# Attention and mixture of experts on one core: maxima ten steps ahead, moved inside SBUF, query rows loaded by half, expert weights and rows apart

## The chip, the cores and the metric

The kernel runs on one core of a Trainium2 chip. The metric is the device time of one execution in microseconds, lower is better.

## The reference, cut to what matters

Layer norm of x (2 x 1024 x 128), then two branches on the normed rows, both added to x: attention with 16 heads of 8 channels whose keys and values come from a latent of 32 channels, and a feed-forward with 16 experts of which each row takes its best two.

```python
def reference(...):
    q = (x @ Wq + bq).reshape(B, S, H, Dh)
    latent = x @ Wl + bl
    k = (latent @ Wk + bk).reshape(B, S, H, Dh)
    v = (latent @ Wv + bv).reshape(B, S, H, Dh)
    scores = jnp.einsum('bihd,bjhd->bhij', q, k) * SCALE
    attn = jax.nn.softmax(scores, axis=-1)
    out = jnp.einsum('bhij,bjhd->bihd', attn, v).reshape(B, S, D) @ Wo + bo
    ...
    top_vals, top_idx = jax.lax.top_k(logits, TOPK)
    gate = jnp.minimum(gate, LIMIT)
    up = jnp.clip(up, -LIMIT, LIMIT)
    gated = (up + 1.0) * gate * jax.nn.sigmoid(gate * ALPHA)
    out_e = jnp.einsum('tef,efh->teh', gated, Wd) + bd[None]
    return x + out + jnp.einsum('teh,te->th', out_e, cw)
```

## The kernel before

Everything is written by hand for the five engines, with semaphores. The sizes: batch 2, 1024 positions, 4 head groups of 4 heads for each batch, so 8 groups. A turn takes two groups; there are 4 turns. A unit is one group and one half (512) of its query positions; it has 8 steps, one for each block of 128 keys. So a turn has 4 units, 32 steps and 16 pairs of steps. The groups alternate between two buffers, q_rows0/k_rows0 (units 0 and 1 of a turn) and q_rows1/k_rows1 (units 2 and 3).

Setup. The projections give q2 and k2, each split into a high and a low part (`low_q`, `low_k`). The first group's rows are copied from them inside SBUF (`first_rows`, L323 ff.: SyncE for q, GpSimd for k). SyncE stores all parts to DRAM (`store_parts`, L393 ff.) and later loads each group from there (`load_group`, L381 ff.). VectorE works out the place of each row among its expert's blocks, GpSimd scatters the rows to a table in DRAM, and SyncE loads blocks of them back (`load_rows`, L374) and the weights of their experts (`load_weights`, L368 to L370, where expert numbers are read from SBUF into registers). Four blocks of 128 rows are a group of blocks; 12 of these are worked through, 4 to a turn.

The two rows with the maxima. Softmax needs each query's maximum before the exponentials. A row tile has 64 partitions, of which 62 hold parts of q and the last 2 (from MAXROW = 62) hold the negative maxima in two parts, against ones in k_rows. So a score product of 64 rows gives score minus maximum. The maxima come from products of 62 rows (`max_job`, L982) that run LEAD steps ahead of the scores, four to a step, through a ring of three PSUM banks: TensorE makes 128 x 512 scores, VectorE reduces them (L818). After the last maximum of a unit VectorE splits the maxima (L822 to L827, tile max2), TensorE turns them (`turn_maxima`, L988), VectorE copies them to maxT (L832), and two DMAs follow: `store_max` (L337) writes maxT to a DRAM buffer, `load_max` (L343) waits for that and loads it into rows 62 and 63 of q_rows. The first score product of a unit waits for this (s_maxin).

The main loop. `pair(p)` on each engine writes out two steps a and b. On TensorE, in this order: scores a0, two maxima, scores a1, a maximum, values of step a - 1 (L999), a maximum, scores b0, a maximum, then the turned blocks and one item of the experts' work (L1068 rows, L1070 gate, L1072 up, L1074 down), a maximum, scores b1, two maxima, values of step a. ScalarE makes an exponential from each of the four scores (L681) and copies the item's result. Pair numbers run from 3 to 18 in each turn's loop (HEAD = 3); 0 to 2 of the first turn stand ahead of it, and 16 to 18 are pairs 0 to 2 of the next turn. The last turn has no items, and its maxima end with the last step. In its pairs 10 to 15 the output projection is written.

What sets the order of the DMAs: SyncE's queue is one list, `turn(t)`, L429 ff. At pair p it has, in this order, the maxima (if a unit's are turned in p), a group load at p = 8 and 16 (it waits for the scores that use the buffer), first-turn weights and stores, and by the table RELOAD the next weights and rows of the experts, where the rows wait for the scatters of the buffer's last results. The first unit's maxima, and those turned in pairs 0 to 2, are moved by ScalarE's queue instead.

```python
LEAD = 12
RELOAD = {HEAD: (-2,), 5: (-1,), 11: (0,), 13: (1,)}
def has_max_turn(p, last):
    return p % 4 == 2 and has_max(p - 1, last)
```

## Time and profile before

| | |
|---|---|
| median of 3 runs | 473.39 us (470.63 to 473.43) |
| the profiled execution | 474.39 us, span 472.6 us |
| busy share of the span | TensorE 93%, VectorE 81%, ScalarE 65%, GpSimd 43% |
| mean granted TensorE clock | 0.94 |
| DMA | 38.05 MB, mean 81 GB/s |

The span is the time from the first to the last instruction on the chip; the execution's own time is a little longer. PE is TensorE, PEld its weight loads, DVE VectorE, ACT ScalarE, POOL GpSimd, SP SyncE; a q behind a name (SPq) means the engine's queue, where DMAs are issued. Matrix products are pipelined and overlap in the records. An engine that is idle costs nothing unless another waits for it.

### The profile page before, as it was taken

Reading aid. Unit: us, or ns where it says so; the run is one execution under the profiler, and the core shown is the slowest. Engines: PE = TensorE matmul, PEld = TensorE weight load, DVE = VectorE, ACT = ScalarE, POOL = GpSimd, SP = SyncE. Lnnn points to the kernel's source line nnn. Section 1 sums busy time; section 2 is a strip of 40 time slices with the busy share of each in tenths; the row PEclk is TensorE's granted clock in tenths of the full one; section 3 lists DMA queues with packets and bytes.
Section 4 is the critical chain, followed back from the end, with each engine's and each line's share of the span. In section 5 each row is a group of like instructions: output and inputs, shape, how many; then the busy total and the mean of one; then the engine's idle time right before and its main releaser. Section 6 shows DMA issues by size and latency. Waiting matters only on the chain.

```text
span 472.6 us, 9064 instructions
## 1 busy us (share of the span) xinstructions
PE 439.6 (93%) x2681; PEld 206.6 (44%) x2681; DVE 381.1 (81%) x757; ACT 309.2 (65%) x356; POOL 204.0 (43%) x238
## 2 busy tenths in 40 slices
PE   0998999989999989999999989999999999999995
PEld 0555444334444435444444444444444443333453
DVE  8559998958888887989898979898989888996112
ACT  1524005558777777787878777788787867676871
POOL 7043787205154543733454527442717274860000
PEclk9968555979999999999999999999999999999999
DMA  5994721464242315060503252513200322400001
GB/s 150 188 151 185 122 59 51 133 188 153 83 111 68 111 48 85 25 186 3 92 17 112 80 86 38 163 35 68 36 6 10 58 33 56 129 3 3 25 22 46
DMA packets 37699, 38.05 MB, mean 81 GB/s; under 512 B 5408, under 2 KB 33158, under 8 KB 36776
## 3 DMA queue, kind: packets, MB, share of 16 engines
q1 hardware_dynamic: 33696, 32.75, 30.4%
q0 software_dynamic: 2944, 4.75, 3.9%
q10 hardware_dynamic: 1032, 0.23, 0.3%
q8 instruction: 12, 0.20, 0.2%
q14 instruction: 15, 0.12, 0.1%
HBM read 23.77 MB, written 13.93 MB: 80 GB/s over the span
## 4 chain that ended last, share of the span: by engine, by line
PE 54%; DVE 18%; DMA 12%; ACT 6%; issue 5%; SPq 4%; ACTq 1%; DVEq 0%
PE banks L999 15%; DVE half_max L818 15%; PE banks L982 13%; PE banks L1051 11%; DMA k_rows<-k_parts 8%; ACT probs L681 5%; PE banks L1070 2%; SPq L389 2%; DMA max_rows<-maxT 2%; PE banks L1072 2%; PE banks L1007 1%; SPq L386 1%; PE banks L940 1%; PE banks L916 1%; DMA y<-in_x 1%
## 5 line engine op out<-in xcount | busy, mean ns | idle before, releaser
L818 DVE TENSOR_REDUCE half_max<-banks 128x1 f32<-128x512 f32 x512 | 322.2, 682 | 41.5 <-PE banks L982 40.1
L681 ACT ACTIVATE probs<-banks 128x1024 f32<-128x1024 f32 x256 | 254.1, 1024 | 122.5 <-PE banks L1051 115.1
L982 PE MATMUL banks<-k_rows,q_rows 62*128 62x512 f32 x512 | 181.5, 469 | 4.1 <-DVE half_max L818 2.4
L1051 PE MATMUL banks<-q_rows,k_rows 64*128 64x512 f32 x512 | 144.1, 460 | 9.8 <-ACT probs L681 3.3
L999 PE MATMUL banks<-probs,v_pad 128*32 128x512 f32 x1024 | 138.1, 612 | 0.1
L982 PEld LDWEIGHTS banks<-k_rows,q_rows 62*128 62x128 f32 x512 | 83.4, 197 | 89.8 <-DVE half_max L818 77.2
L1051 PEld LDWEIGHTS banks<-q_rows,k_rows 64*128 64x128 f32 x512 | 58.1, 189 | 78.8 <-ACT probs L681 63.1
L563 POOL DMA_INDIRECT moe_table<-x_rows,result_row x48 | 48.0, 999 | 64.4 <-ACT x_rows L669 46.9
L533 POOL TENSOR_TENSOR gate<-gate,w_blk 128x512 f32<-128x512 f32 x12 | 12.5, 1044 | 84.8 <-ACT gate L665 84.8
L523 POOL DMA_INDIRECT x_table<-xn,place_u x32 | 31.2, 976 | 22.6 <-DVE place_u L799 13.2
L999 PEld LDWEIGHTS banks<-probs,v_pad 128*32 128x32 f32 x1024 | 20.2, 108 | 43.0 <-issue 29.6
L533 POOL TENSOR_TENSOR up<-up,w_blk 128x512 f32<-128x512 f32 x12 | 12.6, 1047 | 9.4 <-ACT up L667 9.2
L551 POOL TENSOR_TENSOR up<-up,th 128x512 f32<-128x512 f32 x12 | 15.4, 1282 | 1.0
L546 POOL TENSOR_TENSOR th<-th,gate 128x512 f32<-128x512 f32 x12 | 15.3, 1273 | 1.0
L909 PE MATMUL banks<-id_f,xn 128*128 128x128 f32 x16 | 3.8, 412 | 12.5 <-DVE xn L738 12.5
L1070 PE MATMUL banks<-xT_blk,w_blk 128*128 128x128 f32 x96 | 13.9, 288 | 0.0
L1074 PE MATMUL banks<-w_blk,up 128*128 128x128 f32 x96 | 13.7, 286 | 0.0
L1070 PEld LDWEIGHTS banks<-xT_blk,w_blk 128*128 128x128 f32 x96 | 11.6, 191 | 4.4 <-ACT probs L681 4.1
L1074 PEld LDWEIGHTS banks<-w_blk,up 128*128 128x128 f32 x96 | 11.6, 191 | 3.3 <-ACT probs L681 3.3
L858 DVE TENSOR_TENSOR y<-y,banks 128x512 f32<-128x512 f32 x4 | 2.8, 688 | 12.5 <-PE banks L1035 12.5
L1072 PE MATMUL banks<-xT_blk,w_blk 128*128 128x128 f32 x96 | 12.7, 275 | 0.0
L1072 PEld LDWEIGHTS banks<-xT_blk,w_blk 128*128 128x128 f32 x96 | 11.7, 192 | 0.0
(119 smaller groups left out, 300.4 us busy)
## 6 DMA issues: line engine op xcount, KB each, us to landing
w_blk<-in_wexp SPq DMA_DIRECT2D x48, 193.0 KB, 2.7
q_rows<-q_parts SPq DMA_DIRECT2D x28, 128.0 KB
k_rows<-k_parts SPq DMA_DIRECT2D x56, 64.0 KB
x_table<-blank SPq DMA_DIRECT2D x1, 3096.0 KB, 19.9
x_rows<-x_table SPq DMA_DIRECT2D x12, 258.0 KB, 3.8
q_parts<-q SPq DMA_DIRECT2D x8, 256.0 KB
k_parts<-k SPq DMA_DIRECT2D x8, 256.0 KB
y<-in_x SPq DMA_DIRECT2D x4, 256.0 KB, 4.1
```

The lines of the kernel that those rows point to most:

```text
L523: pool.indirect_dma_start(x_table, bass.IndirectOffsetOnAxis(place_u[:, k, t:t + 1], 0), xn[:, t, :], None).then_inc(s_scattered, 16)
L533: mlp(nc.gpsimd.tensor_tensor(dst[:, :, :], dst[:, :, :], w_blk[:, GB * i:GB * i + GB, 2 * P + col:2 * P + col + 1].to_broadcast([P, GB, P ...
L551: nc.gpsimd.tensor_tensor(up[:, :, :], up[:, :, :], th[:, :, :], ALU.mult).then_inc(s_gated, 1)
L563: pool.indirect_dma_start(moe_table, bass.IndirectOffsetOnAxis(result_row[:, i, q:q + 1], 0), x_rows[:, i, q, 0:D], None, bounds_check=2 * ...
L681: nc.scalar.activation(probs[:, (2 * s + part) % 4, :, :], banks[:, bank:bank + 2, :], ACT.Exp, scale=SCALE).then_inc(slot_free, 1)
L818: nc.vector.tensor_reduce(half_max[:, unit, row, half:half + 1], banks[:, ring_bank(job), :], AX_X, ALU.max).then_inc(ring_free, 1)
L982: pe.matmul(bank, q_rows[slot][rows, pair, q0:q0 + P], k_rows[slot][rows, pair, 512 * keys:512 * keys + 512], start=True, stop=True).then_ ...
L999: mm = pe.matmul(banks[32 * j:32 * j + 32, 4, :], v_pad[:, (unit // 2) % 2, kb, j, :], probs[:, (2 * s + j // 2) % 4, j % 2, :], start=(kb ...
L1051: mm = pe.matmul(banks[:, bank + u, :], k_rows[(unit // 2) % 2][rows, pair, P * kb:P * kb + P], q_rows[(unit // 2) % 2][rows, pair, 512 * ...
L1070: mm = pe.matmul(block, w[:, 0:P], xT_blk[:, P * q:P * q + P], start=True, stop=True)
L1072: mm = pe.matmul(block, w[:, P:2 * P], xT_blk[:, P * q:P * q + P], start=True, stop=True)
L1074: mm = pe.matmul(block, up[:, q, :], w[:, 2 * P + 2:3 * P + 2], start=True, stop=True)
```

## The change

LEAD becomes 10. A unit's maxima are turned in the pair with p % 4 == 3, after its third maximum and directly ahead of the values, where before they were turned with p % 4 == 2 after the fifth. They go from maxT straight to q_rows by two DMAs within SBUF (`move_max`), one for each half of the partitions, and the DRAM buffer is gone. The tile q_rows has its half outermost, so that each half is loaded by itself and has its own semaphore (s_q1 for the second). The first group's q rows are copied half by half. TensorE waits for a group's rows one pair later. The weights of the first two groups of blocks are loaded ahead of the wait for the scatters and of the rows. RELOAD is split in two tables, WEIGHTS_IN and ROWS_IN, the rows one or two pairs after the weights. In the first turn, the second unit's maxima are moved by SyncE in pair 3 instead of by ScalarE in pair 2.

```diff
-LEAD = 12
+LEAD = 10
...
-RELOAD = {HEAD: (-2,), 5: (-1,), 11: (0,), 13: (1,)}
+WEIGHTS_IN = {HEAD: -2, 5: -1, 11: 0, 13: 1}
+ROWS_IN = {4: -2, 6: -1, 12: 0, 15: 1}
...
 def has_max_turn(p, last):
-    return p % 4 == 2 and has_max(p - 1, last)
+    return p % 4 == 3 and has_max(p - 1, last)
...
-TURN_OF_FIRST = 4 * KB + 4
+TURN_OF_FIRST = 4 * KB + 2
...
-        q_rows = [sb(f"q_rows{i}", [P, 2, S], F32R) for i in range(2)]
+        q_rows = [sb(f"q_rows{i}", [P, 2, 2, 512], F32R) for i in range(2)]
...
+        def move_max(queue, unit, job):
+
+            parity, slot, half = unit % 2, (unit // 2) % 2, unit % 2
             queue.wait_ge(ring_free, job + 1)
-            queue.dma_start(max_rows[unit % 2], maxT[:, unit % 2, :].bitcast(F32)).then_inc(s_maxout, 16)
-
-        def load_max(queue, unit, done):
-            parity, slot, half = unit % 2, (unit // 2) % 2, unit % 2
-            queue.wait_ge(s_maxout, 16 * done)
             for u in range(2):
-                queue.dma_start(q_rows[slot][64 * u + MAXROW:64 * u + ROWS, :, 512 * half:512 * half + 512].bitcast(F32),
-                                max_rows[parity, 16 * u:16 * u + 16].rearrange("(c j q) t -> c j (q t)", c=PARTS, j=2)).then_inc(s_maxin[parity], 16)
+                queue.dma_start(q_rows[slot][64 * u + MAXROW:64 * u + ROWS, half, :, :].bitcast(F32),
+                                maxT[16 * u:16 * u + 16, parity, :].bitcast(F32)).then_inc(s_maxin[parity], 16)
...
             def load_group(g, slot):
+                for half in range(2):
+                    for u in range(2):
+                        for c in range(PARTS):
+                            r = 64 * u + 2 * DH * c
+                            sp.dma_start(q_rows[slot][r:r + 2 * DH, half, :, :].bitcast(F32).rearrange("r j t -> r (j t)"),
+                                         q_parts[g, u, half].rearrange("a d j t -> (a d) (j t)")).then_inc((s_q1 if half else s_qk)[slot], 16)
+                            for a in range(PARTS * (1 - half)):
+                                sp.dma_start(k_rows[slot][r + DH * a:r + DH * a + DH, :, :].bitcast(F32).rearrange("r j t -> r (j t)"),
+                                             k_parts[g, u, c].rearrange("d j t -> d (j t)")).then_inc(s_qk[slot], 16)
...
             load_group(1, 1)
+            sp.wait_ge(s_expert, 1)
+            load_weights(0)
+            load_weights(1)
             sp.wait_ge(s_scattered, 16 * 2 * TILES)
             for m in range(SLOTS):
                 load_rows(m)
-            sp.wait_ge(s_expert, 1)
-            load_weights(0)
-            load_weights(1)
...
-            store_max(act, 0, TURN_OF_FIRST)
-            load_max(act, 0, 1)
+            move_max(act, 0, TURN_OF_FIRST)
             for p in range(HEAD):
                 pair(0, slots_before(p, 0, False), 0, p, False)
-                if has_max_turn(p, False):
-                    unit = (2 * p + LEAD - 2) // KB
-                    store_max(act, unit, AHEAD_JOBS + jobs_before(p, 0, False) + 5)
-                    load_max(act, unit, unit + 1)
...
-                if p == 2 and isinstance(t, int) and t == 0:
-                    pe.wait_ge(s_qk[1], qk_count(1, 0))
-                if p == 10 and not last:
+                if p == 3:
+                    pe.wait_ge(s_qk[1], qk_count(1, t))
+                if p == 7:
+                    pe.wait_ge(s_q1[1], q1_count(1, t))
+                if p == 11 and not last:
                     pe.wait_ge(s_qk[0], qk_count(0, t + 1))
-                if p == 18:
-                    pe.wait_ge(s_qk[1], qk_count(1, t + 1))
+                if p == 15 and not last:
+                    pe.wait_ge(s_q1[0], q1_count(0, t + 1))
```

The program of TensorE before, in pair 14 of the loop (each L1051 row is a score product, L982 a maximum, L999 values, a REGISTER_ALU row works out a wait's count). The turned maxima (L988) come after the fifth maximum, well behind the values:

```order
L982 MATMUL banks<-k_rows0,q_rows0 128x512 [waits ring_free]
L999 MATMUL banks<-probs,v_pad 32x512 [waits slot_free]
L999 MATMUL banks<-probs,v_pad 32x512 x3
L972 REGISTER_ALU
L982 MATMUL banks<-k_rows0,q_rows0 128x512 [waits ring_free]
L1040 REGISTER_ALU
L1051 MATMUL banks<-q_rows1,k_rows1 128x512 [waits slot_free]
L1051 MATMUL banks<-q_rows1,k_rows1 128x512
L972 REGISTER_ALU
L982 MATMUL banks<-k_rows0,q_rows0 128x512 [waits ring_free]
L986 REGISTER_ALU
L972 REGISTER_ALU [waits s_max2]
```

The row that follows these is the turned block itself, L988. And now, in pair 15 of the changed kernel (L1065 scores, L996 a maximum, L1002 the turned maxima, L1013 values):

```order
L1065 MATMUL banks<-q_rows1,k_rows1 128x512 [waits slot_free]
L1065 MATMUL banks<-q_rows1,k_rows1 128x512
L987 REGISTER_ALU
L996 MATMUL banks<-k_rows0,q_rows0 128x512 [waits ring_free]
L1000 REGISTER_ALU
L987 REGISTER_ALU [waits s_max2]
L1002 MATMUL banks<-id_f,max2 32x128 [waits ring_free]
L1013 MATMUL banks<-probs,v_pad 32x512 [waits slot_free]
L1013 MATMUL banks<-probs,v_pad 32x512 x3
```

The turned block moved from behind the fifth maximum of pair 14 to behind the third of pair 15, ahead of the values, and the unit's first scores stand at the start of pair 16 in both.

SyncE's queue before, at pairs 13 to 16, where x_rows is the experts' rows and max_rows the DRAM buffer:

```order
L370 DMA w_blk<-in_wexp 128x386
L374 DMA x_rows<-x_table 128x4x129 [waits s_res_out1]
L337 DMA max_rows<-maxT 32x128 [waits ring_free]
L343 DMA q_rows<-max_rows 2x2x512 [waits s_maxout]
L343 DMA q_rows<-max_rows 2x2x512
L386 DMA q_rows<-q_parts 16x2048 [waits slot_full]
```

And now:

```order
L380 DMA w_blk<-in_wexp 128x386
L353 DMA q_rows<-maxT 2x8x128 [waits ring_free]
L353 DMA q_rows<-maxT 2x8x128
L384 DMA x_rows<-x_table 128x4x129 [waits s_res_out1]
L398 DMA q_rows<-q_parts 16x1024 [waits slot_full]
```

The rows of the experts, and their wait for the scatters (s_res_out1), moved behind the maxima; one wait (s_maxout) between two DMAs is gone.

ScalarE's queue before, ahead of the loop (the first twelve exponentials are pairs 0 to 2):

```order
L337 DMA max_rows<-maxT 32x128 [waits ring_free]
L343 DMA q_rows<-max_rows 2x2x512 [waits s_maxout]
L343 DMA q_rows<-max_rows 2x2x512
L681 ACTIVATE probs<-banks 128x1024 [waits slot_full] x4
L681 ACTIVATE probs<-banks 128x1024 [waits s_pv,slot_full] x8
L337 DMA max_rows<-maxT 32x128 [waits ring_free]
L343 DMA q_rows<-max_rows 2x2x512 [waits s_maxout]
L343 DMA q_rows<-max_rows 2x2x512
```

And now:

```order
L665 ACTIVATE v_all<-banks 128x4x128 [waits s_v_ps] x4
L353 DMA q_rows<-maxT 2x8x128 [waits ring_free]
L353 DMA q_rows<-maxT 2x8x128
L698 ACTIVATE probs<-banks 128x1024 [waits slot_full] x4
L698 ACTIVATE probs<-banks 128x1024 [waits s_pv,slot_full] x8
```

The three DMAs behind pair 2 left this queue, and the wait for the store with them.

## Rows read from the trace of the kernel before

**Rows 1.** The page: busy time of an engine, share of the span, instructions.

```profile
PE 439.6 (93%) x2681; PEld 206.6 (44%) x2681; DVE 381.1 (81%) x757; ACT 309.2 (65%) x356; POOL 204.0 (43%) x238
```

**Rows 2.** A stretch of the steady part: busy time, granted clock, DMA share, GB/s.

```profile
200.00:220.00 20.00, 19.75 (x134) 8.91 (x134) 18.12 (x34) 16.51 (x20) 8.36 (x10) 1.00 0.39 112
```

**Rows 3.** Waits of TensorE for DMAs: us in all, times, longest.

```profile
PE banks L1051 <- DMA k_rows<-k_parts: 2.9, 5, 0.7
PE banks L1051 <- DMA q_rows<-max_rows: 2.8, 2, 1.4
```

**Rows 4.** ScalarE's timeline (start, length): first exponentials of pairs 2 to 5.

```profile
87.40 1.94 ACT L681 ACTIVATE probs<-banks 128x1024 f32<-128x1024 f32 x2 [1.34 <-PE banks L1051]
...
96.35 2.86 ACT L681 ACTIVATE probs<-banks 128x1024 f32<-128x1024 f32 x3 [3.66 <-DVE half_max L818]
...
103.75 1.94 ACT L681 ACTIVATE probs<-banks 128x1024 f32<-128x1024 f32 x2 [2.08 <-PE banks L1051]
...
110.06 1.94 ACT L681 ACTIVATE probs<-banks 128x1024 f32<-128x1024 f32 x2 [0.71 <-PE banks L1051]
```

**Rows 5.** Timelines of the lead: VectorE's maxima, first maxima moved, first scores.

```profile
43.32 19.22 DVE L818 TENSOR_REDUCE half_max<-banks 128x1 f32<-128x512 f32 x32
...
66.10 0.34 ACTq L337 DMA_DIRECT2D max_rows<-maxT  x1
67.53 1.85 ACTq L343 DMA_DIRECT2D q_rows<-max_rows  x2
...
71.79 1.12 PE L1051 MATMUL banks<-q_rows,k_rows 64*128 64x512 f32 x2
```

**Rows 6.** DMA issues: times, KB each, median us from issue to landing.

```profile
x_rows<-x_table SPq DMA_DIRECT2D x12, 258.0 KB, 3.8
...
k_rows<-k POOLq DMA_DIRECT2D x8, 64.0 KB, 6.4
...
max_rows<-maxT SPq DMA_DIRECT2D x14, 16.0 KB, 1.4
```

**Rows 7.** The chain that ended last, at a late move of maxima.

```profile
171.74 2.70 DMA max_rows<-maxT
...
175.20 2.20 DMA q_rows<-max_rows
```

**Rows 8.** Three us after ScalarE's gap: busy times, granted clock.

```profile
99.00:102.00 3.00, 3.00 (x16) 1.09 (x14) 1.80 (x4) 1.83 (x3) 0.00 (x0) 0.50 0.77 240
```

**Rows 9.** SyncE's queue: first rows and first weights of the experts.

```profile
87.88 2.03 SPq L374 DMA_DIRECT2D x_rows<-x_table  x4
92.66 6.76 SPq L370 DMA_DIRECT2D w_blk<-in_wexp  x8
```

**Rows 10.** SyncE's queue around the late move of maxima.

```profile
171.31 0.38 SPq L374 DMA_DIRECT2D x_rows<-x_table  x1
...
174.46 1.35 SPq L343 DMA_DIRECT2D q_rows<-max_rows  x2
```

**Rows 11.** TensorE in pair 6 of the second turn: start, expert rows, next pair.

```profile
214.30 0.49 PE L1051 MATMUL banks<-q_rows,k_rows 64*128 64x512 f32 x2
...
217.26 0.62 PE L1068 MATMUL banks<-id_f,x_rows 128*128 128x128 f32 x4
...
220.03 0.50 PE L1051 MATMUL banks<-q_rows,k_rows 64*128 64x512 f32 x2
```

**Rows 12.** VectorE in the same pair: five reductions and the copy to maxT.

```profile
215.19 3.08 DVE L818 TENSOR_REDUCE half_max<-banks 128x1 f32<-128x512 f32 x5
218.19 0.27 DVE L832 CAST maxT<-banks 32x128 fp32r<-32x128 f32 x1
```

**Rows 13.** TensorE in the last turn: first scores of pairs 9, 10 and 11.

```profile
426.25 0.49 PE L1051 MATMUL banks<-q_rows,k_rows 64*128 64x512 f32 x2
...
432.18 0.73 PE L1051 MATMUL banks<-q_rows,k_rows 64*128 64x512 f32 x4
...
436.93 0.74 PE L1051 MATMUL banks<-q_rows,k_rows 64*128 64x512 f32 x4
```

122 lines of the change are left out of this document (65 added, 57 removed).

## The prediction

> **What bounds the kernel now.** I read the page first, then the stretches (busy time of each engine in 20 us), the waits, and last the timelines of the places that the waits named. The page has TensorE at 439.6 of 472.6 us [rows 1]. In a stretch of the steady part TensorE is busy 19.75 of 20 us at a full granted clock, VectorE 18.12 and ScalarE 16.51 [rows 2]: TensorE bounds each step, and a step goes faster only if TensorE stops waiting. So I looked for the few waits that TensorE cannot cover. There are three kinds [rows 3]: five waits, 2.9 us in all, for the k rows of the next group; two waits, 2.8 us, for the maxima written into the query rows; and, in ScalarE's timeline, 3.66 us in which it did nothing because DMAs stood in its own queue [rows 4]. Ahead of the steady part lies a lead in which TensorE and VectorE only make maxima, one each 0.60 us, which VectorE sets (32 reductions in 19.22 us) [rows 5]. At the end, pairs of steps without maxima follow, in which VectorE has little to do.
>
> I call two steps a pair (4 score products with their exponentials, 2 value products, 8 maxima); there are 16 pairs to a turn, and a unit is 4 pairs.
>
> **The lead is shorter.** LEAD falls from 12 to 10 steps, so 40 maxima instead of 48 come before the first scores: 8 x 0.60 = 4.8 us less [rows 5]. The first scores stood at 71.79 and would stand at 67.0. But they also wait for the first unit's maxima. These were turned after maximum 36 and are now turned after 34, 1.2 us earlier, so ScalarE's first DMA moves from 66.10 to 64.9. There are now two issues and no round trip through DRAM. The two issues took 1.85 us at this place [rows 5], and I add 1.1 to 1.6 us from the end of the issue until the data are there: the old store's 1.4 us less its issue of 0.3 [rows 5, 6], and the old load's 2.2 less 0.65 [rows 7]. That is 67.9 to 68.4, a wait of about 1.3 us. The term is -3.5 us. Bounds: -4.8 with no wait, -2.8 with a wait of 2 us.
>
> **ScalarE's queue in pair 2.** Before, ScalarE stored the second unit's maxima and waited for the store to land before it could issue the load and go on with the exponentials: it stood from 92.7 to 96.35. Pair 2 took 96.35 - 87.40 = 8.95 us, and pair 3 took 103.75 - 96.35 = 7.40, against 6.31 for pair 4 [rows 4]. Pair 3 was long because TensorE's granted clock was 0.50 in 99 to 102 us, the 1.2 GHz level [rows 8], right after TensorE had stood idle behind ScalarE. Now SyncE moves this unit in pair 3. Both pairs should take what pair 4 took, plus 0.1 for the transposed weights of pair 2: 8.95 + 7.40 - 6.3 - 6.3 gives 3.75, and the term is -3.7 us. Bounds: -4.2 if both come down to 6.1, and -2.2 if the clock still falls once or rows come late (below). What makes this possible on SyncE is the move of the first weights: they were issued only at 92.66, after the rows, and held SyncE for 6.76 us [rows 9]. Now they stand ahead of the wait for the scatters, in time in which SyncE had nothing to do. What may be late next is the first block of rows for the experts. It is still issued at 87.9 [rows 9], because the wait for GpSimd's scatters ends it and GpSimd is not changed; it takes 3.8 us to land [rows 6], so 91.7. Pair 3 now has its first exponential at 87.40 - 3.5 + 6.3 = 90.2 and its first score one score (0.50 us) earlier, at 89.7; TensorE wants the rows 3.0 us into the pair (217.26 less 214.30 in a pair of the same make [rows 11]), at 92.7. That is 1.0 us of room.
>
> **The waits in the steady part.** SyncE issued a max store at 171.74 only after an x_rows load that waited for scatters until 171.31 [rows 10]; the load followed at 174.46 and landed at 177.40, when TensorE already wanted it [rows 7, 10]. In the new order the load of rows for group 1 stands two pairs later and behind the copy of the maxima. The query rows' wait of 2.8 us is gone. The group loads are issued at the same pair as before, but the maxima that need them start at pairs 11 and 3 instead of 10 and 2, a whole pair of about 6 us later. Waits of at most 0.7 us each [rows 3] vanish under that. The four more q copies of each group cost SyncE some 0.3 us of issue each (as much as the store's), and they stand last of the group, in time in which it waits anyway. Term: -5.7 us; bounds -5.9 and -5.0.
>
> **The copy of the maxima has less time now.** This is the new wait. Before, a unit's maxima were turned in the pair after the last maximum and the scores came 1.5 pairs later. Now they are turned in the very pair ahead of the scores. Behind the waiting score stands all of TensorE, and behind it ScalarE and VectorE, so a wait costs its full length. I take pair 6 of the second turn, whose order is the same but for the place of the copy [rows 11, 12]. The pair starts on TensorE at 214.30 and the next at 220.03. VectorE makes five reductions from 215.19 in 3.08 us and then the copy to maxT at 218.19. With only three ahead of it, the copy would end at 215.19 + 1.85 + 0.27 = 217.3. That leaves 2.7 us. The two copies need 0.65 us for the issue of the first (1.35 for two [rows 10]) and then, for the second, 1.4 us (what the store took from issue to landing [rows 6]) to 2.2 us (what the load took [rows 7]): 2.05 to 2.85 us. So the wait is 0 to 0.15 in such a pair, and somewhat more where the pair is shorter. I take 0.1 us each, between the two rows and nearer to the load's, since that one wrote the same two partitions. There are 15 copies after the first (four in each of three turns, three in the last): +1.5 us. Bounds: 0, and 15 x 0.3 = 4.5. The only copies from SBUF to SBUF of this kind in the trace, k_rows from k, took 6.4 us [rows 6], in the busiest stretch for DMA; and one store, issued behind an x_rows load, took 2.7 [rows 7]. These ends are kept for the rivals. The Trainium skill (DMA: Bandwidth & Descriptors, "Anatomy of one DMA") says that a DMA has a fixed part of about 2.0 us, most of it the receipt of the last write, heaviest for HBM. By that rule, the second copy would land 0.65 + 2.0 = 2.65 us after the copy, just in time, and the term would be 0; the store's 1.4 us in this trace is shorter still.
>
> Placing the transpose ahead of the values costs nothing more: the values stand behind it in either engine's shadow, and its ring place is freed after the same count of maxima.
>
> **The end.** The 8 maxima that left the lead come back in pair 10 of the last turn. On TensorE this pair took 436.93 - 432.18 = 4.75 us, and the pair before it, with maxima and a turned value block, 432.18 - 426.25 = 5.93 [rows 13]. Pair 10 becomes like it: +1.2, and 0.1 for the copy now in pair 11, so +1.3 us. Bounds +0.9 and +1.8.
>
> **Sum.** -3.5 - 3.7 - 5.7 + 1.5 + 1.3 = -10.1 us. The profiled execution took 474.39 us of its own, 472.6 of it span; 1.8 us lie around the span and do not change. That gives 464.3. The median of the runs shown is 1.0 below the profiled one, so 463.3 us is the forecast. With every term at its good bound: -4.8 - 4.2 - 5.9 + 0 + 0.9 = -14.0, or 459.4; at its bad bound: -2.8 - 2.2 - 5.0 + 4.5 + 1.8 = -3.7, or 469.7.
>
> **Rivals.** (A) Slower: the copy lands late at every unit. If two copies between partitions of SBUF take as long after the turn as the old store and load together (1.4 + 0.65 + 2.2 = 4.3 us), TensorE waits 4.3 - 2.7 = 1.6 us at 15 places, 24 us, against 11.6 us gained elsewhere: +12.4, some 486 us. It decides from 11.6 / 15 = 0.77 us of wait, that is from a landing 3.5 us after VectorE's copy. For it speaks the 6.4 us of k_rows from k; against it, that these were eight DMAs of 64 KB on GpSimd's queue beside eight of 64 KB on SyncE's, and here stand two of 8 KB alone. Chance 0.08.
>
> (B) The copy lands 0.5 us late each time: 7.5 instead of 1.5 us, so -4.1 and 469.3 us. That is a second copy of 2.55 us, close to the store that took 2.7 [rows 7]. The new copies are cut into 16 pieces of 128 elements where the old load had four of 512, and this could lengthen them beyond both rows used. The Trainium skill (DMA: Bandwidth & Descriptors, "Why a DMA increments its semaphore by 16 and not by 1") says that such a DMA runs on the largest number of engines, up to 16, that divides the outer size of both sides; here that is 2, so eight pieces would queue on each of two engines. No row of the trace shows this. Chance 0.18.
>
> (C) The head gives nothing in pairs 2 and 3: the rows of the first group come later than 3.8 us (four loads of 258 KB are issued together), TensorE stands, and its clock falls as it did at 97 us. Then -10.1 + 3.7 = -6.4, 467.0 us. For it: 1.0 us of room only. Chance 0.14.
>
> The forecast keeps 0.60.
>
> **How the numbers follow.** The range must leave out no more than 2 in 10: A lies outside, and so does a small part of B, and 459 to 471 holds the rest. About 1% (4.7 us) is what a measurement of this kernel can tell from no change. Faster than 468.7: nearly all of the forecast, most of C and a third of B, 0.77. Within 1%: the rest of B and a little of the others, 0.14. Slower: A and a share for a wait between B and A, 0.09.
>
> **What would show it.** In the trace after: the first scores near 68.3 instead of 71.79; pairs 2 and 3 at 6.3 us each and no granted clock of 0.50 near 99; no wait of TensorE for k_rows from k_parts after pair 3; the waits for the copy of maxima at most 0.3 us each, and 1.5 us in all; pair 10 of the last turn near 5.9 us. The forecast is wrong if the row "scores <- DMA q_rows<-maxT" stands at 7 us or more, or if pairs 2 and 3 together take over 14 us.

## The result, and the profile after

The changed kernel takes 469.9 us (median of 20 runs, 466.52 to 471.6) beside 473.36 us of the kernel before in runs on the same chips (20 runs, 469.25 to 476.22): a ratio of 0.9931, 95% interval 0.991 to 0.9952. That is 3.3 us faster. The forecast was 463.3, 10.1 us faster. The profiled execution took 470.34 us, 468.6 of it span, 4.0 less than the span before. So the sign was right, two thirds of the gain are missing, and the question is where they went.

The page of the changed kernel, engines, and the granted clock in its 40 slices:

```profile
PE 434.6 (93%) x2681; PEld 202.3 (43%) x2681; DVE 379.0 (81%) x757; ACT 308.8 (66%) x356; POOL 204.4 (44%) x238
...
PEclk9978557999999999999999999999999999999997
```

TensorE's share is what it was [rows 1], with as many instructions. The page hides the answer: an engine that is 93% busy before and after can have traded one stall for another. The waits name the trade. TensorE's waits of the changed kernel (us in all, times, longest):

```profile
PE banks L1002 <- DVE half_max L830: 5.9, 14, 0.6
PE banks L1065 <- ACT probs L698: 3.0, 17, 0.3
PE banks L996 <- DVE half_max L830: 1.6, 2, 1.4
PE banks L1035 <- DVE half_max L830: 1.1, 1, 1.1
PE banks L1002 <- DVE max L839: 1.0, 2, 0.8
PE banks L1065 <- DMA q_rows<-maxT: 0.9, 1, 0.9
```

Both DMA waits of before [rows 3] are gone, 5.7 us. The copy of the maxima, on which my doubts had been, is waited for once, 0.9 us. New is the first row: the turned maxima (L1002) wait 14 times for VectorE's reductions, 5.9 us.

Where the time goes is best read from four stretches, cut at the first exponential of a pair in ScalarE's timeline: up to pair 5 of the first turn, from there to pair 10 of the last turn, from there to pair 15 of the last turn, and the rest. The stretches in us (span's start is 0):

| Kernel | first exponential | to pair 5 | steady | end | rest | span |
|---|---|---|---|---|---|---|
| before | 72.94 | 110.06 | 322.65 | 25.23 | 14.7 | 472.6 |
| changed | 69.13 | 101.75 | 323.41 | 27.82 | 15.6 | 468.6 |
| difference | -3.8 | -8.3 | +0.8 | +2.6 | +0.9 | -4.0 |
| forecast | -3.5 | -7.1 | -4.4 | +1.4 | 0 | -10.1 |

(The forecast's terms fall on the stretches so: of the fifteen copies at 0.1 us, one in the first stretch, thirteen in the steady one, one at the end.) The head did what was forecast and 1.2 us more. The steady part, which was to win 4.4 us, lost 0.8. The end cost 1.2 us more than forecast, and 0.9 us came at the very last.

The head first. ScalarE's timeline of the changed kernel, the exponentials that open pairs 1 to 5:

```profile
76.82 1.94 ACT L698 ACTIVATE probs<-banks 128x1024 f32<-128x1024 f32 x2 [2.00 <-PE banks L1065]
...
83.45 1.94 ACT L698 ACTIVATE probs<-banks 128x1024 f32<-128x1024 f32 x2 [1.32 <-PE banks L1065]
...
89.53 1.94 ACT L698 ACTIVATE probs<-banks 128x1024 f32<-128x1024 f32 x2 [1.43 <-PE banks L1065]
...
95.97 1.94 ACT L698 ACTIVATE probs<-banks 128x1024 f32<-128x1024 f32 x2 [0.72 <-PE banks L1065]
...
101.75 1.02 ACT L698 ACTIVATE probs<-banks 128x1024 f32<-128x1024 f32 x1 [0.71 <-PE banks L1065]
```

Against [rows 4], pair 2 went from 8.95 to 89.53 - 83.45 = 6.08 us and pair 3 from 7.40 to 6.44. The 3.66 us in which ScalarE stood are gone, and so is the low clock; the windows of the changed kernel for 96 to 99 and 99 to 102 us (busy times, granted clock, DMA share, GB/s) answer to [rows 8]:

```profile
96.00:99.00 3.00, 3.00 (x24) 1.42 (x21) 2.86 (x5) 3.00 (x4) 0.00 (x0) 1.00 0.48 138
99.00:102.00 3.00, 3.00 (x23) 1.48 (x22) 2.31 (x5) 2.20 (x4) 1.67 (x2) 1.00 0.69 202
```

The granted clock is 1.00, the 2.4 GHz level, where it had been 0.50.

Now the steady part. The timeline of the changed kernel in pair 7 of the second turn, a pair with turned maxima (PE, PEld and DVE rows, and SyncE's queue):

```profile
211.61 0.50 PE L1065 MATMUL banks<-q_rows,k_rows 64*128 64x512 f32 x2
...
212.46 1.89 DVE L830 TENSOR_REDUCE half_max<-banks 128x1 f32<-128x512 f32 x3
213.21 0.09 PEld L1002 LDWEIGHTS banks<-id_f,max 128*32 128x32 f32 x1 [0.84 <-DVE half_max L830]
213.21 0.28 PE L1002 MATMUL banks<-id_f,max 128*32 128x128 f32 x1 [0.39 <-DVE half_max L830]
213.42 1.07 PE L1013 MATMUL banks<-probs,v_pad 128*32 128x512 f32 x8
214.27 0.27 DVE L844 CAST maxT<-banks 32x128 fp32r<-32x128 f32 x1
...
214.56 1.39 SPq L353 DMA_DIRECT2D q_rows<-maxT  x2
...
218.06 0.50 PE L1065 MATMUL banks<-q_rows,k_rows 64*128 64x512 f32 x2
```

The pair takes 218.06 - 211.61 = 6.45 us; before, pair 7 of the second turn took 5.77 (226.42 less 220.65 in ScalarE's timeline). The values (L1013) begin 213.42 - 211.61 = 1.81 us into the pair. The turned block ahead of them wants a place in the ring of banks (`ring_free`), which VectorE frees by reducing a maximum, and VectorE begins on this pair's maxima only at 212.46, so the block stands 0.39 us and then takes its own 0.21. The values want nothing from VectorE; they stand behind it only because the queue is in order.

One of each kind of the pairs that hold the turned block now (3, 7, 11 and 15 of each turn), in us:

| Kernel | pair 3, turn 2 | pair 7, turn 2 | pair 11, turn 2 | pair 15, turn 1 |
|---|---|---|---|---|
| before (no turned block there) | 5.98 | 5.77 | 5.79 | 7.25 (with its DMA wait) |
| changed | 6.98 | 6.47 | 6.45 | 6.46 |

So each costs about 0.7 us more than a free pair (pair 3 of the second and third turn 1.0), and 13 of them lie in the steady stretch, some 9 us. Against that stand the waits that are gone and what the block had cost in the pairs that it left (pair 14 of the second turn fell from 6.09 to 5.71 us).

### The profile page after: what moved, and what is told of

Read it like the earlier page. It is cut to its first block, busy times and chain, and to the rows that moved or that the text cites. A ratio compares the mean times of both kernels' runs of the same rounds, so it can differ in the third digit from the quotient of the medians.

```text
span 468.6 us, 9086 instructions
## 1 busy us (share of the span) xinstructions
PE 434.6 (93%) x2681; PEld 202.3 (43%) x2681; DVE 379.0 (81%) x757; ACT 308.8 (66%) x356; POOL 204.4 (44%) x238
## 4 chain that ended last, share of the span: by engine, by line
PE 64%; DVE 18%; ACT 9%; issue 6%; DMA 2%; ACTq 0%; SPq 0%; DVEq 0%
PE banks L1013 21%; PE banks L996 15%; DVE half_max L830 14%; PE banks L1065 13%; ACT probs L698 7%; PE banks L1084 3%; PE banks L1086 2%; PE banks L1021 2%; PE banks L931 1%; ACT th L690 1%; PE banks L1049 1%; DMA y<-in_x 1%; PE banks L955 1%; PE banks L1002 1%; PE banks L938 1%
## 5 line engine op out<-in xcount | busy, mean ns | idle before, releaser
L996 PE MATMUL banks<-k_rows,q_rows 62*128 62x512 f32 x512 | 175.2, 457 | 3.6 <-DVE half_max L830 1.6
L1065 PE MATMUL banks<-q_rows,k_rows 64*128 64x512 f32 x512 | 142.3, 457 | 4.6 <-ACT probs L698 3.0
L1013 PE MATMUL banks<-probs,v_pad 128*32 128x512 f32 x1024 | 137.2, 608 | 0.1
L996 PEld LDWEIGHTS banks<-k_rows,q_rows 62*128 62x128 f32 x512 | 80.2, 195 | 86.0 <-DVE half_max L830 72.5
L1065 PEld LDWEIGHTS banks<-q_rows,k_rows 64*128 64x128 f32 x512 | 57.6, 187 | 73.2 <-ACT probs L698 62.1
L550 POOL TENSOR_TENSOR gate<-gate,w_blk 128x512 f32<-128x512 f32 x12 | 12.5, 1045 | 79.4 <-ACT gate L682 79.4
L1013 PEld LDWEIGHTS banks<-probs,v_pad 128*32 128x32 f32 x1024 | 20.2, 108 | 38.8 <-issue 22.3
L924 PE MATMUL banks<-id_f,xn 128*128 128x128 f32 x16 | 4.1, 432 | 12.5 <-DVE xn L750 12.5
```

What stands on the lines that cost most here:

```text
L550: mlp(nc.gpsimd.tensor_tensor(dst[:, :, :], dst[:, :, :], w_blk[:, GB * i:GB * i + GB, 2 * P + col:2 * P + col + 1].to_broadcast([P, GB, P ...
L996: pe.matmul(bank, q_rows[slot][rows, half, pair, P * qb:P * qb + P], k_rows[slot][rows, pair, 512 * keys:512 * keys + 512], start=True, st ...
L1013: mm = pe.matmul(banks[32 * j:32 * j + 32, 4, :], v_pad[:, (unit // 2) % 2, kb, j, :], probs[:, (2 * s + j // 2) % 4, j % 2, :], start=(kb ...
L1065: mm = pe.matmul(banks[:, bank + u, :], k_rows[(unit // 2) % 2][rows, pair, P * kb:P * kb + P], q_rows[(unit // 2) % 2][rows, half, pair, ...
```

## The experiments

All ratios are to the kernel before on the same chip, with 95% intervals. Four kernels ran beside each other in each batch.

**The turned block behind the values.** The one change to the changed kernel is the order of two pieces of TensorE's code; VectorE's order, the DMAs and LEAD stay.

```diff
-                if has_max_turn(p, last):
-                    unit = (2 * p + LEAD - 2) // KB
-                    turn_maxima(jbase, job, unit, 4 * t + unit + 1)
-                    job += 1
                 if p > 0:
                     values(sbase, slot, t, a - 1)
+                if has_max_turn(p, last):
+                    unit = (2 * p + LEAD - 2) // KB
+                    turn_maxima(jbase, job, unit, 4 * t + unit + 1)
+                    job += 1
```

> The changed kernel with one edit: TensorE's turned maxima stand behind the values product instead of ahead of it (the order of VectorE's work is the same). Theory T (the turned block waits for VectorE to free its ring bank, and the ready values stand behind it; about 0.65 us in each of 15 pairs): the pairs before a unit's first scores fall from 6.46 to about 5.8 us, 15 x 0.6 = 9 us less than the changed kernel, a ratio to the kernel before of about 0.974. Theory C (the copy of the maxima lands late and the scores wait for it): the copy is not earlier, so nothing is gained, ratio 0.993, and a wait of scores for the copy shows. Theory V (VectorE is the bound of these pairs, with 8 reductions, the split of the maxima and the copy): the wait only moves to the next maximum, ratio 0.99 or above.

Measured: 466.13 us, ratio 0.9876 (0.9851 to 0.9901), against 0.9931 for the change itself. TensorE and SyncE in pair 7 of the second turn of this kernel:

```profile
211.36 0.50 PE L1065 MATMUL banks<-q_rows,k_rows 64*128 64x512 f32 x2
...
212.50 1.06 PE L1013 MATMUL banks<-probs,v_pad 128*32 128x512 f32 x8
213.49 0.10 PEld L1002 LDWEIGHTS banks<-id_f,max 128*32 128x32 f32 x1 [0.84 <-DVE half_max L830]
213.50 0.28 PE L1002 MATMUL banks<-id_f,max 128*32 128x128 f32 x1
...
214.31 1.39 SPq L353 DMA_DIRECT2D q_rows<-maxT  x2
...
217.57 0.49 PE L1065 MATMUL banks<-q_rows,k_rows 64*128 64x512 f32 x2
```

The values begin 1.14 us into the pair, TensorE does not stand at L1002 (its weight load shows an idle time, its matmul none), and the pair takes 6.21 us. The expectation had the mechanism of theory T right and its size too large: it wanted pairs of 5.8 us and a ratio of 0.974. The steady stretch is 318.95 us, 4.5 less than in the changed kernel and 3.7 less than before: the forecast of -4.4 holds for it within 0.7. The span of the profiled execution is only 3.7 less than the changed kernel's, since the head gave 1.1 back. Two waits of TensorE there (columns as above):

```profile
PE banks L1065 <- DMA q_rows<-maxT: 2.1, 2, 1.5
...
PE banks L1082 <- DMA x_rows<-x_table: 0.8, 1, 0.8
```

The first unit's copy is waited for 1.54 us instead of 0.86, and the expert rows in pair 3, the place where I had counted 1.0 us of room, came 0.8 us late.

**The turned block behind the fifth maximum of the same pair.** VectorE's order changes with TensorE's: five maxima, then the turned block.

```diff
-                for n, (ahead, m) in enumerate(maxima[:3]):
+                for n, (ahead, m) in enumerate(maxima[:5]):
...
-                for n, (ahead, m) in enumerate(maxima[3:5]):
-                    max_job(base, job + n, ahead, m, t)
-                job += len(maxima[3:5])
```

> The changed kernel with the turned maxima behind the fifth maximum of the same pair, as the kernel before has it, one pair nearer to the scores. Theory T: the wait at the turned block goes (gain 9 us), but VectorE's copy comes about 1.2 us later, near 4.1 us after the pair's start, and the two DMAs need 2 to 2.8 us, so the first scores of a unit wait 0.4 to 1.2 us for the copy: 6 to 18 us back, ratio 0.985 to 1.01, with a row of scores waiting for the copy of some 15 times. Theory V: 0.993 or above, with VectorE never idle in these pairs.

Measured: 477.19 us, ratio 1.012 (1.0087 to 1.0152), slower than before. The ring wait is down to 0.2 us once, and a DMA wait is there instead (the wait, and the place in pair 7 of the second turn):

```profile
PE banks L1062 <- DMA q_rows<-maxT: 16.4, 15, 1.3
```

```profile
217.94 0.27 DVE L844 CAST maxT<-banks 32x128 fp32r<-32x128 f32 x1
...
218.24 1.39 SPq L353 DMA_DIRECT2D q_rows<-maxT  x2
...
221.05 0.50 PE L1062 MATMUL banks<-q_rows,k_rows 64*128 64x512 f32 x2 [1.05 <-DMA q_rows<-maxT]
```

Here the copy's length shows, as it does not where nothing waits for it: 221.05 - 218.21 = 2.84 us from the end of VectorE's copy to the scores. My range was 2.05 to 2.85. The Trainium skill (DMA: Bandwidth & Descriptors, "Anatomy of one DMA") has a fixed part of about 2.0 us, which that section states for DMAs issued by GpSimd. With the first copy's issue added, the estimate from it was 2.65; this row, on SyncE's queue, is 0.2 us above it. The DMA engines' own records of these two copies show where the time goes. Each copy is 16 pieces of 512 bytes that run two at a time (in the windows 219.55 to 219.80 and 220.25 to 220.52 the DMA share is 0.12 and 0.11 of 16 engines, and 0.00 between them). Those of the first copy run from 219.56 to 219.79 and those of the second from 220.26 to 220.50, each followed by two writes of 4 bytes. So moving the data takes 0.24 us for each copy, 1.3 us pass between SyncE's first issue and the first piece, and 0.55 us between the last piece and TensorE's scores. So the place behind the fifth maximum, which served with 1.5 pairs of time, doesn't serve with half a pair; and in the changed kernel the copy has 218.06 - 214.54 = 3.5 us, 0.7 more than it needs.

**Everything but LEAD and the place.** LEAD is 12 again, the block is turned behind the fifth maximum of pairs with p % 4 == 2, and the waits for the groups stand at pairs 2, 6, 10, 14 and 18. The direct copies, the halves, the early weights and the split tables stay. ScalarE moves the second unit in pair 2, by the direct copies.

```diff
-LEAD = 10
+LEAD = 12
...
-    return p % 4 == 3 and has_max(p - 1, last)
+    return p % 4 == 2 and has_max(p - 1, last)
```

> The changed kernel with maxima 12 steps ahead and the turned maxima at their old place (pair p % 4 == 2, behind the fifth maximum), the group waits back at pairs 2, 10 and 18; the move inside SBUF, the halves, the early weights and the split tables stay. Theory T: the head of pairs 2 and 3 (3.7 us) and the two late moves (2.8 us) stay gained, the lead of 3.8 us and part of the group waits (1 to 3 us) are lost, no wait at the turned block: 474.4 - 6.5 = 468, ratio 0.984 to 0.99, so as good as or better than the changed kernel. Theory V: the same place costs what it costs there, and without the shorter lead it is 3 us slower than the changed kernel, ratio 1.0.

Measured: 465.75 us, ratio 0.9863 (0.9837 to 0.989), the fastest of its batch, 0.4 us ahead of the first experiment, which the two intervals do not tell apart. No wait for a DMA is left in TensorE's waits at all. Pair 7 of the second turn takes 5.79 us again, the steady stretch 318.46, the end 25.21, as long as before. It begins 3.5 us later than the changed kernel (first exponential at 72.68) and has that back by the end of the steady part. ScalarE, not SyncE, moves the second unit here, and pairs 2 and 3 still take 6.39 + 5.84 = 12.2 us, as short as in the changed kernel (12.5) and 4.1 less than before. So the move to SyncE is not what shortens these pairs: without the store and the wait for it, ScalarE's queue serves as well.

**The kernel before, with the block turned early.** This is the mirror of the first experiment: in the kernel before, the block goes behind the third maximum and ahead of the values, and nothing else changes.

```diff
-                for n, (ahead, m) in enumerate(maxima[:5]):
+                for n, (ahead, m) in enumerate(maxima[:3]):
```

(VectorE's side; on TensorE's, `turn_maxima` moves ahead of `values`.)

> The kernel before with one edit: the turned maxima stand behind the third maximum, ahead of the values, in the same pair as before (p % 4 == 2). Theory T: the pairs with a turned block grow from 5.73 to about 6.4 us, 15 times 0.65 = 9 to 10 us more, ratio 1.02; a wait of the turned block for VectorE of about 0.4 us each. Theory C: nothing changes or it gets up to 1 us faster, ratio 1.0, since the moved maxima are ready earlier.

Measured: 479.79 us, ratio 1.0161 (1.0133 to 1.0188). Its steady stretch is 329.53 us, 6.9 more than before; pair 6 of the second turn takes 6.45 us where it took 5.73. The wait is that of the changed kernel:

```profile
PE banks L991 <- DVE half_max L818: 9.5, 14, 0.9
```

So the placement alone costs 6.3 to 8.9 us (the interval of the ratio) in a kernel that has nothing else of the change. That is net: four of the five waits for k_rows of before [rows 3] are gone from it (one of 0.7 us is left), so the block's place costs somewhat more than the total shows.

**The turned block behind the fourth maximum.** It was meant to find a place between too early and too late: values, fourth maximum, turned block.

```diff
+                if maxima:
+                    max_job(jbase, job, a + LEAD, 3)
+                    job += 1
                 if has_max_turn(p, last):
```

> The changed kernel with the turned maxima one maximum later still (values, fourth maximum, turned maxima, second score). VectorE's copy comes 0.6 us later than with the turned maxima behind the values (e1), where 3.3 us were left and 2.8 needed. Theory T with a copy of 2.8 us: the wait at the turned block is gone as in e1, and the first scores of a unit wait 0.1 to 0.3 us for the copy: equal to e1 within 3 us, 1 to 3 us below the changed kernel. If the copy needs more: the scores wait 0.6 us or more, 15 times, ratio 0.997 or above.

Measured: 469.95 us, ratio 0.9964 (0.9933 to 0.9996), beside 470.08 and 0.9965 (0.9938 to 0.9993) for the changed kernel in the same batch: no gain. The ring wait is gone, TensorE waits for copies six times, 2.3 us in all and 0.6 at most, and pair 7 of the second turn, where it waits for nothing of the kind, takes 6.39 us all the same. TensorE and VectorE in the second half of that pair:

```profile
214.46 1.16 PE L1084 MATMUL banks<-xT_blk,w_blk 128*128 128x128 f32 x8
...
215.54 0.49 PE L996 MATMUL banks<-k_rows,q_rows 62*128 62x512 f32 x1
...
216.08 1.89 DVE L830 TENSOR_REDUCE half_max<-banks 128x1 f32<-128x512 f32 x3 [0.82 <-PE banks L996]
```

VectorE stands 0.82 us, because the next maximum lies behind 1.16 us of expert work on TensorE. Pairs 7, 11 and 15 hold this item (1.16 us), where pairs 6, 10 and 14, in which the block stood before, hold a lighter one (0.62 us [rows 11]). That could be why the block costs 0.4 to 0.6 us in pair 7 even where nothing makes it wait, but it is not all: in the last turn, which has no items, pair 7 takes 5.77 us with the block behind the values and 5.43 without it. No run moved the items, so this rest stays open.

**First weights late again.** In the changed kernel the first two groups' weights go back behind the scatters' wait and the rows. It ran twice, since the first chip had a disturbance of its own (below).

```diff
-            sp.wait_ge(s_expert, 1)
-            load_weights(0)
-            load_weights(1)
             sp.wait_ge(s_scattered, 16 * 2 * TILES)
             for m in range(SLOTS):
                 load_rows(m)
+            sp.wait_ge(s_expert, 1)
+            load_weights(0)
+            load_weights(1)
```

> The changed kernel with the first two weight loads put back behind the first rows and their wait for the scatters. If the early weights are what lets SyncE move the second unit's maxima in pair 3: SyncE is then busy with eight weight loads until about 99 us, so the copy for pair 4 is issued 5 to 7 us late, pair 3 of the first turn takes 10 us or more instead of 6.4, and the clock may fall for some us behind it: 4 to 9 us slower than the changed kernel, ratio to the kernel before 1.002 to 1.012. Rival: the weights are quick and the order does not matter, ratio 0.993.

> The kernel of e5_weights_late again; there all engines stood 7 us in pair 1 of the head, so that SyncE had caught up before pair 3 and the question stayed open. If the early weights are what lets SyncE move the second unit's maxima in time: with no such stand, the eight weight loads run from 90 to 97 us, the copy is issued near 97 instead of 92.5, and pair 3 takes 9 us or more instead of 6.4: 3 to 9 us above the changed kernel. If the order does not matter: equal to the changed kernel.

Measured: 481.44 us, ratio 0.9822 (0.9791 to 0.9854), in the second batch; 478.83 us, ratio 1.0143 (1.0091 to 1.0195), in the third, where the changed kernel had 0.9965. The third batch is clear: without the early weights the change is slower than before by more than it is now faster. SyncE's queue and TensorE in pair 3 of that run, and the windows (as above):

```profile
87.04 2.04 SPq L384 DMA_DIRECT2D x_rows<-x_table  x4
...
91.81 6.74 SPq L380 DMA_DIRECT2D w_blk<-in_wexp  x8
...
98.59 1.45 SPq L353 DMA_DIRECT2D q_rows<-maxT  x2
102.16 0.79 PE L1065 MATMUL banks<-q_rows,k_rows 64*128 64x512 f32 x2 [7.60 <-DMA q_rows<-maxT]
```

```profile
99.00:102.00 3.00, 0.00 (x0) 0.00 (x0) 0.00 (x0) 0.00 (x0) 0.00 (x0) 0.59 0.53 150
102.00:105.00 3.00, 2.84 (x11) 1.38 (x15) 1.59 (x3) 1.93 (x2) 0.00 (x0) 0.50 0.31 79
```

The copy of the second unit stands behind the weights' 6.74 us of issue, TensorE waits 7.60 us, and its clock then falls to 0.50, the 1.2 GHz level, as it did before behind ScalarE's stand [rows 8].

**The rows with the weights; the halves together.** Two small edits take single parts of the change back. The first lets ROWS_IN be as RELOAD was, in the changed kernel; the second lets the LEAD 12 kernel wait for both halves of a group at once.

```diff
-ROWS_IN = {4: -2, 6: -1, 12: 0, 15: 1}
+ROWS_IN = {HEAD: -2, 5: -1, 11: 0, 13: 1}
```

```diff
                 if p == 10 and not last:
                     pe.wait_ge(s_qk[0], qk_count(0, t + 1))
+                    pe.wait_ge(s_q1[0], q1_count(0, t + 1))
```

(and the same at pair 18)

> The changed kernel with the experts' rows loaded in the same pairs as their weights again (3, 5, 11, 13). My prediction put 2.8 us of gain to the late moves of maxima, which the split of the tables and the direct move remove together. If the split is needed: the wait for the scatters at pair 13 holds SyncE until about the middle of pair 15, the copy is late at pair 16 in the first two turns, 1 to 1.5 us each, ratio 0.998. If the direct move and its later place are enough (the scatters land before the copy to maxT is made): no change, ratio 0.993.

> The kernel of e3_lead12 with TensorE waiting at pairs 10 and 18 for both halves of the query rows (the order of SyncE's loads stays: first half and k rows, then second half). If loading by half is what took the waits of 0.7 us at these pairs away: waits of 0.5 to 1.5 us come back at up to 6 places, 3 to 6 us more, ratio 0.993 to 0.998. Rival: the waits went because SyncE's queue was freed earlier, ratio 0.986 as before.

Measured: 483.57 us, ratio 0.9875 (0.9841 to 0.9908), and 478.98 us, ratio 0.9784 (0.9732 to 0.9836). All four kernels of this batch, and the kernel before in it (490.18 us), ran on a chip on which pair 5 began 10 to 12 us later than elsewhere, so I read their pairs and not their ratios. With the rows back at their old pairs, pair 15 of the first turn still takes 6.43 us as in the changed kernel (6.46), not 7.25: the split table is not what took that wait away. In SyncE's queue x_rows is issued at 174.70 and the copies at 176.22, right behind VectorE's copy to maxT, which ends at 176.20: at the place that the maxima have now, the wait for the scatters is over 1.5 us before they are ready. With the halves waited for together, pair 9 of the first turn takes 6.19 us, not 6.86 as before, and no wait for the group is in the trace: waiting by halves is not needed for that either. What took the five waits of 0.7 us away in the LEAD 12 kernel, I can't say from one run: the group's load, from SyncE's issue until the DMA engines fall quiet, went from about 13 us (from 224.7) to about 12 (from 217.8), and that is all that I see.

**The projection later.** PROJECT is moved off pair 10 of the last turn, on top of the first experiment. In this kernel the third block's turned rows overwrite those of the second before they are projected, with the same number of instructions.

```diff
-PROJECT = {10: (0, 0), 12: (0, 1), 14: (1, 0)}
+PROJECT = {11: (0, 0), 13: (0, 1), 14: (1, 0)}
```

> The changed kernel with the turned maxima behind the values (as in e1_turn_behind_values) and the first two blocks of the output projection one pair later (pairs 11 and 13 instead of 10 and 12), so that pair 10 of the last turn, which has 8 maxima again, does not also wait for VectorE to free all of them before the turned rows of attention. If that wait is the excess of the end (pair 10 took 6.9 us, 1.0 more than I forecast, and pair 11 0.45 more): pairs 10 and 11 together fall from 12.6 to about 11.4, 1.0 to 1.5 us less than e1, ratio 0.985. Rival: VectorE's total work sets the end, nothing gained, 0.9876.

Measured: 479.6 us, ratio 0.9786 (0.9761 to 0.9811), in the disturbed batch. From the start of pair 10 to that of pair 15 in the last turn it took 27.54 us, against 27.60 in the first experiment. Pairs 10 and 11 fell from 12.60 us to 10.37, and pairs 12 to 14 rose from 15.00 to 17.17. The stall in pair 10 can be moved, not won.

**The changed kernel and the LEAD 12 kernel again.**

> The changed kernel itself, beside the three others of this group on one chip, so that they can be set against each other. Ratio to the kernel before 0.993, as measured, and 15 pairs of 6.45 us or more.

> The kernel of e3_lead12 (all of the change but LEAD and the place of the turned maxima), again, beside the changed kernel. If the new place costs more than the shorter lead brings: 3 to 4 us below the changed kernel, ratio to before 0.986. If the difference of the first comparison was between chips: no difference.

Measured side by side: 470.08 us, ratio 0.9965 (0.9938 to 0.9993), and 464.95 us, ratio 0.9855 (0.9816 to 0.9894). The LEAD 12 kernel beats the kernel before on two chips, and beats the changed one by 5.1 us on this one; on the other the ratios to the kernel before say the same (0.9863 against 0.9931). On this chip the change itself is worth 1.6 us.

The stretches of all undisturbed kernels, as above:

| Kernel | first exponential | to pair 5 | steady | end | rest |
|---|---|---|---|---|---|
| before | 72.94 | 110.06 | 322.65 | 25.23 | 14.7 |
| changed | 69.13 | 101.75 | 323.41 | 27.82 | 15.6 |
| behind the values | 69.66 | 102.83 | 318.95 | 27.60 | 15.5 |
| behind the fifth maximum | 68.94 | 102.08 | 330.63 | 27.77 | 14.6 |
| behind the fourth | 68.62 | 101.42 | 322.83 | 27.58 | 15.5 |
| LEAD 12 | 72.68 | 104.98 | 318.46 | 25.21 | 15.2 |
| LEAD 12 again | 72.91 | 103.77 | 318.51 | 25.25 | 14.7 |
| before, turned early | 73.11 | 107.99 | 329.53 | 25.04 | 14.6 |

## Why the prediction was wrong

**The step that failed** is the sentence "Placing the transpose ahead of the values costs nothing more: the values stand behind it in either engine's shadow, and its ring place is freed after the same count of maxima." The count is the same, but not the time. This term of the sum was put at nothing, and the runs show it at 4.5 us: the block now asks for its place about 0.9 us earlier in the pair than behind the values (1.21 us into it; 213.50 less 211.36 is 2.14 in the first experiment), before VectorE, which first splits the old maxima, has reduced one of the new ones. TensorE stands 0.4 us, 14 times, and the block's own time comes before the values too. The order of TensorE alone, swapped back, gives 4.5 us in the steady stretch; put into the kernel before, it costs 6.9 there. With it behind the values, the stretch wins 3.7 us, near the forecast 4.4. Of the difference of 5.2 us between forecast and measurement in this stretch, that is 4.5. I had the pair's order in front of me (the rows of both engines at that place) and looked only at who waits for the copy, not at what the block itself waits for. Neither sign of being wrong that the prediction names appeared (the row of waits for the copy stands at 0.9 us, and pairs 2 and 3 take 12.5 us together), and the measured time lies beyond the sum with every term at its bad bound (469.7), though most terms came as forecast: a cost that no term held could not be seen by either.

**The copy of the maxima**: the mechanism and its length were right. I gave it 2.05 to 2.85 us and 2.7 us of time; it takes 2.8. It waits nowhere in the steady part, because the pair grew by 0.7 us, not because the copy is shorter. At the old pair length of 5.7 it would, by these numbers, have come about 0.1 us late, which was my number; no run shows that pair. Rival B (0.5 us late, a forecast of 469.3, which lies by the result) gave the right time for the wrong reason: the loss per pair was of that size, but it was the ring's, and the copy had 0.7 us to spare. Its doubt about the 16 pieces is answered by the DMA records above: they do run two at a time, and take 0.24 us. Rival A is refuted by the same rows. It would have taken a place behind the fifth maximum to bring it about: there the copies came 1.0 to 1.3 us late and the kernel was slower than before, past the 0.77 us from which I had said that it decides.

**The lead**: forecast -3.5, measured -3.8 in the first exponential and -3.5 in the first scores, which stood at 68.30 (forecast 67.9 to 68.4) after a wait of 0.86 for the copy (forecast about 1.3).

**ScalarE's queue and the early weights**: forecast -3.7 for pairs 2 and 3, measured 16.35 - 12.52 = -3.8, and pair 4 fell from 6.31 to 5.78 as well. Rival C is refuted in the changed kernel. Its mechanism is real, though: in the run with the block behind the values, the rows came 0.85 us late at just that place, the copy then 0.55 us late, and pair 3 took 7.27 us. The 1.0 us of room was counted from an issue at 87.9, since GpSimd is not changed. But the end of the scatters moves between executions: the rows were issued at 88.55 in the changed kernel, at 89.79 in this run, and between 87.04 and 89.79 in the undisturbed ones. That the early weights make SyncE's move possible is shown: without them, pair 3 took 14.39 us. That the move to SyncE was needed is not: the kernel with LEAD 12 has the same gain with ScalarE.

**The steady waits**: forecast -5.7. They are gone, in the changed kernel as in those with LEAD 12. But the reasons that I gave for them, the later wait for the group and the rows two pairs later, are not needed for it, since they stay away with LEAD 12's earlier waits and, at the new place of the maxima, with the old table of rows. For the query rows the direct copy may be enough by itself. TensorE in pair 16 of the first turn before, where the late maxima were waited for:

```profile
177.52 0.51 PE L1051 MATMUL banks<-q_rows,k_rows 64*128 64x512 f32 x2 [1.39 <-DMA q_rows<-max_rows]
```

It wanted them at 177.52 - 1.39 = 176.13. Two direct copies issued in place of the store at 171.74 [rows 7] would have been there near 171.74 + 2.8 = 174.5, an estimate; no run has the old place, the old table and the direct copies together.

**The end** was mis-sized: forecast +1.3 (+1.4 in the table, since the sum counts the copy in pair 11 among the 15 as well), measured +2.6. Pair 10 of the last turn went from 4.76 to 6.88 us, not to 5.9. TensorE's timeline of the changed kernel there:

```profile
427.10 0.40 PE L996 MATMUL banks<-k_rows,q_rows 62*128 62x512 f32 x1
428.63 0.66 PE L1035 MATMUL banks<-id_f,attn 128*128 128x128 f32 x4 [1.14 <-DVE half_max L830]
429.22 0.49 PE L996 MATMUL banks<-k_rows,q_rows 62*128 62x512 f32 x1
```

The pair that I compared it with [rows 13] has no turned attention rows (L1035). These ask for a ring place too, and with maxima in the pair they wait 1.14 us for VectorE. It is the same error as in the steady part: a block of the ring was costed by its own time. With LEAD 12 the wait is not there. Set against the kernel with LEAD 12, the changed one is 3.2 us ahead at pair 5 in one pair of executions and 2.3 in the other (101.48 against 103.77), and gives 2.6 back at the end. No run changes LEAD alone, but so far as these show it, the shorter lead wins next to nothing.

**The last us**: the last projection took 2.07 us instead of 1.16, at a granted clock of 0.50 instead of 1.00. Windows of the changed kernel (464 to 468 us) and TensorE's row:

```profile
463.02 2.07 PE L1049 MATMUL banks<-wo_sb,attnT 128*128 128x128 f32 x8 [0.78 <-DVE attnT L863]
```

```profile
464.00:468.00 4.00, 1.09 (x6) 0.80 (x4) 0.69 (x1) 0.00 (x0) 0.00 (x0) 0.50 0.22 66
```

I don't count it to the change: the same LEAD 12 kernel has some of it in one execution (rest 15.2 us) and none in the other (14.7), with the same idle times ahead of it. The changed kernel has it in both of its executions, the kernel before in neither of its kind (14.7 and, turned early, 14.6), so whether the change makes it more frequent stays open.

In sum: -10.1, with +5.2 in the steady part (4.5 of it the block's place), +1.2 at the end and +0.9 in the last us, and -1.2 that the head gave beyond the forecast, is -4.0, by which the span fell.

## What to carry to other kernels

When a block of work is moved earlier in a queue that runs in order, ask first what the block itself waits for, a free buffer above all, and when that comes in the new place; then count everything behind it. If a step's result is needed sooner, try the place just behind the work that needs nothing from the same engine: here the order of two adjacent pieces of one engine's code was worth 4.5 us of the steady stretch, more than the whole change gained. And a shorter lead is worth its gain less what the same work costs where it comes back; here 2.3 to 3.2 us against 2.6.

## What the runs showed of the hardware

Two direct copies of 8 KB between partitions of SBUF, issued one behind the other by SyncE in 1.39 us, took 2.84 us until TensorE could go on. Only 0.24 us of it for each copy was the moving of the data. The only such copies with a landing time in the trace of before took 6.4 us [rows 6]; they were of 64 KB and stood in the busiest stretch for DMA.

On the chip of the second batch the kernel before took 490.18 us, 18 more than on the others, and pair 5 of the four kernels there began 10 to 12 us late; all of that lies ahead of pair 2. Several engines stood at the same time for 7 us, and the releasers name no DMA and no engine. ScalarE and VectorE of the kernel with late weights:

```profile
87.94 1.29 DVE L830 TENSOR_REDUCE half_max<-banks 128x1 f32<-128x512 f32 x2 [7.07 <-remote]
87.99 1.02 ACT L698 ACTIVATE probs<-banks 128x1024 f32<-128x1024 f32 x1 [7.50 <-remote]
```

From pair 2 on, the pairs that I compared have the lengths that they have elsewhere, to 0.05 us. Not all pairs do: pairs 3 and 4 of the second and third turn together are 0.4 to 1.5 us longer there in each of the four kernels (in the second turn 13.31 us against 11.83 in the kernel with LEAD 12), and the steady stretches 0.8 to 2.4 us. So whether waiting for both halves costs something in those pairs can't be read from this batch. A stand in the head also hides what it delays: in this batch the kernel with late weights waited 0.6 us for the copy, not 7.6, and seemed to be as good as the change. What the engines stood for stays open, and so does whether it is the chip.
